# Conditioned attention and a gated low-rank FFN: folding the conditioning weight into the projections and running attention over pairs of batches

## The chip, the cores and the metric

The kernel runs on one core of one Trainium2 chip. The metric is device time in microseconds (us), the median of several runs; less is better. A profile is one execution taken by the hardware profiler. Its engines are PE (TensorE; PEld is its weight load), DVE (VectorE), ACT (ScalarE), POOL (GpSimd) and SP (SyncE, which issues most transfers).

## What is computed

Eight batches of 256 tokens of 1024 features, all in f32. Every batch has its own low-rank adapter (rank 16) of the conditioning layer and its own matrix for the FFN input:

```python
h = x @ W.T + b + (x @ A[i]) @ Bm[i] * 2          # conditioning, i = itok_B_0_23[batch]
q, k, v = h @ w_q, h @ w_k, h @ w_v               # 32 query heads, 8 key heads, head size 32
o = softmax(q @ k.T / sqrt(32)) @ v
x = x + o @ w_o
g = x @ cond2[j].T                                # j = itok_B_3_7[batch]
x = x + top2_gated_low_rank(g)                    # 4 experts of rank 16, router on g
```

The products that matter run on f32 split into two parts, hi and lo (each rounded to the matmul's f32r format), as hi*hi + hi*lo + lo*hi: three products of TensorE for one. ScalarE writes the hi part by a copy, VectorE the lo part by a subtraction. P = 128 partitions, KT = 8 tiles of 128 features, G = 8 groups of 4 query heads that share a key head.

## The kernel before

It has three stages, each with an instruction stream for every engine; an engine goes through its stream in order and waits at semaphores.

**tokens_stage** computes h for pairs of batches, 512 tokens at a time: `products` (L259) multiplies 8 x 8 weight tiles with x, three times, 192 products of 512 columns per pair. `psU` (L281) is the adapter's first factor, `low_rank` (L265) its second. ScalarE adds the bias while it copies h out (L212), SP stores it to h_scratch in DRAM. The q, k and v weights are split meanwhile.

**attend_stage** goes over batches b and, in each, over the 8 groups g: step n = 8b + g. `project` (L646, L643 for v) multiplies h of one batch (256 columns) with a weight block of 128 columns ("unit": q0 to q7, k0, k1, v0, v1) in 24 products, through two PSUM banks. In step n TensorE issues: the first half of q unit g, scores 0 and 1 of step n-1, the second half, scores 2 and 3 of n-1, then transposed scores and outputs of earlier steps and the turn (a small transposition of the row maxima). k0 stands at the head of step 0, v0 and v1 at the end of step 2, k1 at the end of step 3. The stages of a step are:

- `scores` (L661): q times k, by rows of queries, only for the row maxima; VectorE's `maxima` (L578) reduces them. The two banks make score tile i wait for the maximum of tile i-2.
- the negated maxima are turned (L694), copied (L525) and laid by SP (L445) into rows 96 and 97 of q_stack, so that `scores_t` (L673), two steps later, yields transposed scores less the maximum, which ScalarE exponentiates (`exp`, L508).
- `outputs` (L687): probabilities times v, and times ones for the denominators; `copy_o` (L595) copies both to SBUF; SP stores them to o_scratch and den_scratch.
- q is held as a stack of 32 rows each: hi (`copy_q`, L500, ScalarE), lo (L568, VectorE) and hi again (L572, VectorE); k likewise (L480, L550, L486). h of the next batch is loaded and split (L411, L418) in the steps of this one.

**finish_stage** goes over batches. Denominators are loaded together, inverted (L987), stored, and loaded again per batch, broadcast, as o_scale (L832); `scale_o` (L977) multiplies o with them, `scale_hi` and `scale_lo` split it. `w_o_tile` (L1124) is the output projection, `cond_row` (L1139) multiplies router and expert matrices into cond2, the rest (psX, psY) is the gated FFN. The W_o weights are split in the last steps of attention (`ahead_scalar`, `ahead_vector`, steps s = 4 to 7 of the last batch), through a ring of three buffers that VectorE frees.

Of the kernel before, what the change touches and what calls it, by code (L numbers as in the profile page):

```python
# [7 lines left out]
P = 128  # L29
# [8 lines left out]
E = 4  # L38
# [14 lines left out]
RING = 3  # L53
W_TILES = KT
QKV_TILES = NQKV // P
WO_TILES = KT


def f(ap):

    return ap.bitcast(F32)


class Weights:


    def __init__(self, nc, sb, sem):
        self.nc = nc
        self.raw = sb("weight_raw", [P, RING, D])
        self.landed = [sem(f"weight_landed{i}") for i in range(RING)]  # L70
        self.hi_done = sem("weight_hi_done")
        self.lo_done = sem("weight_lo_done")

    def load(self, eng, n, src):
        if n >= RING:
            eng.wait_ge(self.lo_done, n - RING + 1)
        dst = self.raw[:, n % RING]
        if len(src.shape) == 3:
            dst = dst.rearrange("p (k c) -> p k c", c=src.shape[2])
        eng.dma_start(dst, src).then_inc(self.landed[n % RING], 16)  # L80

    def split_hi(self, act, n, hi):
        act.wait_ge(self.landed[n % RING], 16 * (n // RING + 1))
        self.nc.scalar.activation(hi, self.raw[:, n % RING], ACT.Copy).then_inc(self.hi_done, 1)

    def split_lo(self, dve, n, hi, lo):
        dve.wait_ge(self.hi_done, n + 1)
        dve.tensor_tensor(lo, self.raw[:, n % RING], f(hi), ALU.subtract).then_inc(self.lo_done, 1)  # L88
# [6 lines left out]
def tokens_stage(nc, sem, weights, wq, ahead, load_qkv, xT, idx, WT, bias, lora_A, lora_B, hT):  # L95

    SLOTS = 4
    BANK = [0, 1, 2, 3, 4, 5, 6, 3]
    AB_DMAS = 8
    st = Stage()  # L100
    with ExitStack() as ctx:
        def sb(name, shape, dt=F32):
            return ctx.enter_context(nc.sbuf_tensor(name, shape, dt))

        sb("qkv_head", [P, 4, 2, D])
        w_hi, w_lo = sb("w_hi", [P, KT, D], F32R), sb("w_lo", [P, KT, D], F32R)
        x_raw = sb("x_raw", [P, KT, T2])
        x_hi, x_lo = sb("x_hi", [P, KT, T2], F32R), sb("x_lo", [P, KT, T2], F32R)
        idx_sb = sb("idx_sb", [1, B], I32)
        bias_sb = sb("bias_sb", [P, KT])  # L110
        a_raw = sb("a_raw", [P, 2, KT, R])
        a_hi, a_lo = sb("a_hi", [P, 2, KT, R], F32R), sb("a_lo", [P, 2, KT, R], F32R)

        b_raw = sb("b_raw", [96, 2, D])
        b_stack = sb("b_stack", [96, 2, D], F32R)
        u_stack = sb("u_stack", [96, 2, T], F32R)
        h_out = sb("h_out", [P, SLOTS, T2])
        psH = ctx.enter_context(nc.psum_tensor("psH", [P, 7, T2], F32))
        psU = ctx.enter_context(nc.psum_tensor("psU", [P, T2], F32))

        idx_landed, bias_landed = sem("idx_landed"), sem("bias_landed")
        x_landed = [sem(f"x_landed{k}") for k in range(KT)]
        ab_landed = sem("ab_landed")
        zeroed = sem("zeroed")
        x_hi_done, x_lo_done, x_used = sem("x_hi_done"), sem("x_lo_done"), sem("x_used")
        ab_hi_done, ab_lo_done = sem("ab_hi_done"), sem("ab_lo_done")
# [8 lines left out]
    def both(ap):  # L135
        return ap.rearrange("p (b t) -> p b t", b=2)

    def sync(sp):
        def load_x(pair, k):
            sp.dma_start(both(x_raw[:, k]), xT[bass.ds(2 * pair, 2), :, k].rearrange("b p t -> p b t")  # L140
                         ).then_inc(x_landed[k], 16)
# [1187 lines left out]
```

## Time and profile before

| | us |
|---|---|
| median of 3 runs | 1232.97 (1232.5 to 1234.92) |
| the profiled execution | 1233.04 |
| its span | 1231.4 |
| PE busy | 1136.6 (92%) |
| DVE busy | 720.4 (59%) |
| ACT busy | 475.1 (39%) |
| 16 DMA engines | 120.26 MB, 98 GB/s on average |

The span runs from the first to the last instruction; 1.6 us lie around it. The token stage takes the first 228 us, attention goes to 889, the finish to the end. Busy PE is not PE at its peak, since products are pipelined and overlap in the records: the pace of a row of products is better read from the distance of their starts.

### The profile page before, as it was taken

To read this page: it belongs to the slowest core of one execution; us is meant where nothing else is said; L and a number is where in the kernel's file an instruction comes from. 1 tells how busy PE (TensorE), PEld (TensorE's weight loads), DVE (VectorE), ACT (ScalarE), POOL (GpSimd) and SP (SyncE) were. 2 spreads that over 40 slices of the span, in tenths; PEclk is the share of its full clock that TensorE was granted. 3 is DMA by queue.
4 is the path that set the end of the run, shared out by engine and by line. 5 is a ranking of instruction groups with operands and counts; after the bars stand their busy time and mean duration, and the time that the engine had idled before them with its cause. 6 is when DMAs were issued, how large, how long until landed. Compare 5 with 4: busy or idle time off the path is not lost.

```text
span 1231.4 us, 23057 instructions
## 1 busy us (share of the span) xinstructions
PE 1136.6 (92%) x8592; PEld 911.4 (74%) x8592; DVE 720.4 (59%) x1434; ACT 475.1 (39%) x911; POOL 55.4 (5%) x99
## 2 busy tenths in 40 slices
PE   6999999788998999989989899897689999999996
PEld 5788888676776766767667677674379898988895
DVE  5212122467767677676776767767546666566663
ACT  4223123445445454453454544544322322232320
POOL 2000001100000000000000000001011111111100
PEclk9999999899999999999999999998799999999998
DMA  9341423410100101001010010003486866677530
GB/s 298 96 120 56 133 70 102 137 57 33 54 11 15 52 14 48 14 14 48 18 48 14 14 48 19 23 14 125 145 270 172 240 205 208 177 244 224 190 103 35
DMA packets 60418, 120.26 MB, mean 98 GB/s; under 512 B 8660, under 2 KB 43860, under 8 KB 56276
## 3 DMA queue, kind: packets, MB, share of 16 engines
q1 hardware_dynamic: 47124, 71.41, 19.0%
q0 software_dynamic: 13248, 48.24, 12.4%
q8 instruction: 29, 0.48, 0.2%
q14 instruction: 17, 0.14, 0.0%
HBM read 93.41 MB, written 25.69 MB: 97 GB/s over the span
## 4 chain that ended last, share of the span: by engine, by line
PE 62%; ACT 13%; DVE 11%; issue 7%; DMA 5%; SPq 1%; ACTq 0%; DVEq 0%; POOL 0%; POOLq 0%
PE psW L1124 13%; PE psH L259 13%; PE psP L646 9%; PE psG L1139 7%; ACT q_stack L500 5%; ACT probs L508 5%; PE psP L643 4%; PE psS L661 4%; DVE nmax L578 4%; PE psO L687 4%; PE psT L673 3%; DMA o_scale<-rden_scratch 3%; PE psX L1161 2%; DVE o_sb L595 2%; PE psU L281 2%
## 5 line engine op out<-in xcount | busy, mean ns | idle before, releaser
L646 PE MATMUL psP<-h_hi,wq 128*128 128x256 f32 x1280 | 259.8, 289 | 22.5 <-DVE h_lo L418 16.3
L646 PEld LDWEIGHTS psP<-h_hi,wq 128*128 128x128 f32 x1280 | 210.1, 193 | 46.4 <-issue 25.4
L508 ACT ACTIVATE probs<-psT 128x512 f32<-128x512 f32 x256 | 138.9, 594 | 248.4 <-PE psT L673 247.0
L1124 PE MATMUL psW<-wq 128*128 128x256 f32 x1536 | 197.6, 284 | 0.0
L1124 PEld LDWEIGHTS psW<-wq 128*128 128x128 f32 x1536 | 191.6, 191 | 5.3 <-issue 0.6
L578 DVE TENSOR_REDUCE nmax<-psS 128x2 f32<-128x512 f32 x256 | 164.4, 684 | 41.7 <-PE psS L661 40.9
L646 PE MATMUL psP<-h_lo,wq 128*128 128x256 f32 x640 | 181.8, 284 | 0.0
L568 DVE TENSOR_TENSOR q_stack<-psP,q_stack 32x256 fp32r<-32x256 f32 x256 | 107.4, 419 | 102.3 <-ACT q_stack L500 100.5
L932 ACT ACTIVATE cond_hi<-cond_raw 128x1024 fp32r<-128x1024 f32 x64 | 66.8, 1056 | 165.3 <-PE psG L1139 165.3
L661 PE MATMUL psS<-k_stack,q_stack 96*128 96x256 f32 x512 | 98.7, 303 | 29.6 <-DVE nmax L578 25.2
L646 PEld LDWEIGHTS psP<-h_lo,wq 128*128 128x128 f32 x640 | 123.4, 193 | 0.0
L1004 DVE TENSOR_TENSOR cond_lo<-cond_raw,cond_hi 128x1024 fp32r<-128x1024 f32 x64 | 77.6, 1223 | 71.2 <-ACT cond_hi L932 71.2
L259 PE MATMUL psH<-x_hi,w_hi 128*128 128x512 f32 x256 | 101.9, 398 | 9.6 <-DVE w_lo L88 9.3
L661 PEld LDWEIGHTS psS<-k_stack,q_stack 96*128 96x128 f32 x512 | 73.7, 194 | 46.5 <-DVE nmax L578 35.9
L259 PE MATMUL psH<-x_lo,w_hi 128*128 128x512 f32 x256 | 100.8, 394 | 0.0
L259 PE MATMUL psH<-x_hi,w_lo 128*128 128x512 f32 x256 | 100.7, 394 | 0.0
L500 ACT ACTIVATE q_stack<-psP 32x256 fp32r<-32x256 f32 x256 | 95.7, 374 | 6.7 <-PE psP L646 3.3
L673 PE MATMUL psT<-q_stack,k_stack 98*128 98x512 f32 x256 | 90.6, 435 | 4.6 <-ACT probs L508 2.8
L687 PE MATMUL psO<-probs,v_sb 128*32 128x256 f32 x1024 | 73.3, 406 | 0.9 <-DVE o_sb L595 0.9
L687 PE MATMUL psO<-probs,ones 128*32 128x256 f32 x1024 | 70.5, 394 | 0.0
L673 PEld LDWEIGHTS psT<-q_stack,k_stack 98*128 98x128 f32 x256 | 40.5, 196 | 34.1 <-ACT probs L508 28.5
L259 PEld LDWEIGHTS psH<-x_hi,w_hi 128*128 128x128 f32 x256 | 48.7, 190 | 22.3 <-issue 10.7
(101 smaller groups left out, 1360.8 us busy)
## 6 DMA issues: line engine op xcount, KB each, us to landing
cond_raw<-in_cond POOLq DMA_DIRECT2D x64, 512.0 KB, 4.6
x_raw<-in_xT SPq DMA_DIRECT2D x32, 256.0 KB, 5.2
h_scratch<-h_out SPq DMA_DIRECT2D x32, 256.0 KB, 2.5
act_raw<-h_scratch SPq DMA_DIRECT2D x8, 1024.0 KB, 4.9
o_scratch<-o_sb SPq DMA_DIRECT2D x64, 128.0 KB
act_raw<-o_scratch SPq DMA_DIRECT2D x8, 1024.0 KB, 6.5
o_scale<-rden_scratch SPq DMA_DIRECT2D x32, 256.0 KB, 9.4
x_sb<-in_xT SPq DMA_DIRECT2D x8, 1024.0 KB, 6.9
```

The lines of the kernel that those rows point to most:

```text
L259: mm = pe.matmul(psH[:, BANK[m]], w[:, k, cols], x[:, k], start=(first and i == 0), stop=False)
L500: ins = nc.scalar.activation(q_stack[0:32, g % 4, h], psP[32 * h:32 * h + 32, bank, 0:T], ACT.Copy)
L508: nc.scalar.activation(probs[:, g % 2, i % 2, (i // 2) * 512:(i // 2 + 1) * 512], psT[:, i % 2], ACT.Exp, scale=ATT_SCALE).then_inc(exp_do ...
L568: ins = dve.tensor_tensor(q_stack[32:64, g % 4, h], psP[32 * h:32 * h + 32, bank, 0:T], f(q_stack[0:32, g % 4, h]), ALU.subtract)
L578: dve.tensor_reduce(nmax[:, g % 2, 2 * hp:2 * hp + 2, qt], psS[:, i % 2].rearrange("p (h k) -> p h k", h=2), AX.X, ALU.max, negate=True).t ...
L646: mm = pe.matmul(out, wq[:, u, w, k * P:(k + 1) * P], h[:, k], start=first, stop=end)
L661: mm = pe.matmul(psS[:, i % 2, j * T:(j + 1) * T], q_stack[0:96, g % 4, 2 * hp + j, qt * P:(qt + 1) * P], k_stack[0:96, g], start=True, st ...
L673: pe.matmul(psT[:, kt], k_stack[0:98, g, kt * P:(kt + 1) * P], q_stack[0:98, g % 4, 2 * hp:2 * hp + 2].rearrange("p h t -> p (h t)"), star ...
L687: mm = pe.matmul(psO[HD * h:HD * h + HD, hp], ones[:] if hp else v_sb[:, kt, g], probs[:, g % 2, kt, h * T:(h + 1) * T], start=(kt == 0), ...
L1004: dve.tensor_tensor(cond_lo[:, k % SPLIT], cond_raw[:, k % RAW], f(cond_hi[:, k % SPLIT]), ALU.subtract).then_inc(cond_lo_done, 1)
L1124: mm = pe.matmul(out, wq[:, k, w, m * P:(m + 1) * P], o_part(c, o)[:, k], start=(k == 0 and i == 0), stop=(k == KT - 1 and i == 2))
L1139: mm = pe.matmul(psG[0:EC, half], a[:, k], w[:, k % SPLIT, half * 512:(half + 1) * 512], start=(k == 0 and i == 0), stop=(k == KT - 1 and ...
```

## The change

The conditioning is linear, so it is folded into the projection weights. `fold_stage` replaces tokens_stage: it computes W' = W.T times the joined q, k and v weights (1024 x 1536) in three chunks of 512 columns, writes it split into `wq`, and multiplies the second factors of all 8 adapters (8 x 16 = 128 rows) and the bias with the same weights. These small results go through DRAM (b_scratch, bb_scratch).

`attend_stage` now takes x of a pair of batches (512 columns), loaded and split once, and projects it with W'. Each unit ends with one more product, the low-rank part and the bias (`b_stack` times `u_stack`); `project_u` computes u, x times the adapters' first factors. There are 4 pairs of 16 steps; step n handles group g = (n mod 16) // 2 of batch c = n mod 2. `WORK` lists the projection pieces of each step: the first list stands at the head of the step, the second before scores 2 and 3; "a" and "b" are halves of a unit, "+" means the next pair. A unit is finished once its last piece is. Scores of step n, transposed scores of n-1 and outputs of n-2 are in the same step. The third part of the q and k stacks is filled by a transfer (`double`) and no longer by an engine. `normalise` inverts the denominators and multiplies on VectorE each step, so that den_scratch, rden_scratch and o_scale go. The finish is otherwise as it was, unrolled; W_o is loaded whole in the last steps, and split in steps N-2 to N+1, two tiles a step.

The core of the diff (units' copies of u and v, placement in memory, semaphores and removed functions are left out):

```diff
+            load_q(0, k)
+            sp.dma_start(w_raw[:, k], W[k * P:(k + 1) * P]).then_inc(w_landed[k], 16)
+            if k == 0:
+                sp.dma_start(idx_sb[:], idx).then_inc(idx_landed, 16)
+                sp.dma_start(idx2_sb[:], idx2).then_inc(idx_landed, 16)
...
+        for j in range(CHUNKS):
+            if j + 1 < CHUNKS:
+                sp.wait_ge(acc_done, 2 * KT * (j + 1))
+                for k in range(KT):
+                    sp.wait_ge(b_used, KT * j + k + 1)
+                    load_q(j + 1, k)
...
+            if j + 1 < CHUNKS:
+                for k in range(KT):
+                    split_q(j + 1, k)
+            else:
+                ahead(act, True)
+            act.wait_ge(b_used, KT * (j + 1))
+            if j:
+                act.wait_ge(bp_stored, 32 * j)
...
+    def tensor(pe):
+        for j in range(CHUNKS):
+            for k in range(KT):
+                if j == 0:
+                    pe.wait_ge(w_lo_done, k + 1)
+                pe.wait_ge(q_lo_done, KT * j + k + 1)
+                for m in range(KT):
+                    if j and k == 0:
+                        if m < 6:
+                            pe.wait_ge(tile_lo, KT * (j - 1) + m + 3)
+                        elif m == 6:
+                            pe.wait_ge(bp_done, j)
+                        else:
+                            pe.wait_ge(brow_done, j)
+                    for i, (w, q) in enumerate(((w_hi, q_hi), (w_hi, q_lo), (w_lo, q_hi))):
+                        mm = pe.matmul(psF[:, bank(j, m)], w[:, k, m * P:(m + 1) * P], q[:, k],
+                                       start=(k == 0 and i == 0), stop=(k == KT - 1 and i == 2))
+                    if k == KT - 1:
+                        mm.then_inc(tile_done, 1)
+                if j == CHUNKS - 1 and k < KT - 1:
+                    mm.then_inc(w_used, 1)
+            if j == 0:
+                pe.wait_ge(bt_lo_done, 1)
+            pe.wait_ge(tile_lo, KT * j + 1)
+            for k in range(KT):
+                for i, (b, q) in enumerate(((bt_hi, q_hi), (bt_hi, q_lo), (bt_lo, q_hi))):
+                    mm = pe.matmul(psF[:, bank(j, 0)], b[:, k].rearrange("p b r -> p (b r)"), q[:, k],
+                                   start=(k == 0 and i == 0), stop=(k == KT - 1 and i == 2))
+                mm.then_inc(b_used, 1)
+            if j == 0:
+                pe.wait_ge(ones_set, 1)
+            pe.wait_ge(tile_lo, KT * j + 2)
+            pe.wait_ge(acc_done, 2 * KT * (j + 1))
+            pe.matmul(psF[0:2, bank(j, 1)], ones[:, 0:2], acc[:], start=True, stop=True).then_inc(bias_done, 1)
+    st.sync, st.gpsimd, st.scalar, st.vector, st.tensor = sync, gpsimd, scalar, vector, tensor
...
+WORK = [
+    (["v0"], ["v1"]),
+    (["q1"], []),
+    (["v2"], ["v3"]),
+    (["q2"], []),
+    (["q3a"], []),
+    (["q3b"], ["k1a"]),
+    (["k1b"], ["q4a"]),
+    (["q4b"], []),
+    (["q5a"], []),
+    (["q5b"], []),
+    (["q6a"], []),
+    (["q6b"], []),
+    (["q7a"], []),
+    (["q7b"], ["+u"]),
+    (["+k0"], ["+q0a"]),
+    (["+q0b"], []),
+]
...
+        def double(p, u):
+            j = int(u[1:] or 0)
+            if u[0] in "qk":
+                sp.wait_ge(proj_act, unit(p, u) + 1)
+            if u[0] == "q":
+                sp.dma_start(f(q_stack[64:96, j % 2]), f(q_stack[0:32, j % 2])).then_inc(q_dup[j % 2], 16)
+            elif u[0] == "k":
+                sp.dma_start(f(k_stack[32:64, :, 4 * j:4 * j + 4]),
+                             f(k_stack[0:32, :, 4 * j:4 * j + 4])).then_inc(k_dup[j], 16)
...
+        def copy_heads(p, u, to):
+            act.wait_ge(proj_done, unit(p, u) + 1)
+            for h in range(HG):
+                ins = nc.scalar.activation(to(h), both(psP[32 * h:32 * h + 32, bank(p, u)]), ACT.Copy)
+                if h == 1:
+                    ins.then_inc(half_hi, 1)
+            ins.then_inc(proj_act, 1)
...
+        def lows(p, u, to, hi):
+            for h in range(HG):
+                if h == 0:
+                    dve.wait_ge(half_hi, 10 * p + [v for v in SEQ if v[0] in "qk"].index(u) + 1)
+                if h == 2:
+                    dve.wait_ge(proj_act, unit(p, u) + 1)
+                ins = dve.tensor_tensor(to(h), both(psP[32 * h:32 * h + 32, bank(p, u)]), f(hi(h)), ALU.subtract)
+            ins.then_inc(proj_dve, 1)
...
+        def normalise(n):
+            dve.wait_ge(pv_done, n + 1)
+            dve.reciprocal(rden[:], psO[:, 1]).then_inc(rden_done, 1)
+            if n >= 2:
+                dve.wait_ge(o_stored[n % 2], 16 * (n // 2))
+            dve.wait_ge(rden_done, n + 1)
+            dve.tensor_tensor(o_sb[:, n % 2], psO[:, 0], rden[:], ALU.mult).then_inc(o_copied, 1)
...
+        def step(n):
+            p, s = n // STEPS, n % STEPS
+            for part in range(2):
+                for unit_ in finished(n, part):
+                    evacuate(*unit_)
+                if part == 0 and s == 13 and p + 1 < PAIRS:
+                    for k in range(4, KT):
+                        split_x_lo(dve, p + 1, k)
+                if n < N:
+                    maxima(n, 2 * part)
+                    maxima(n, 2 * part + 1)
+            if n < N:
+                split_maxima(n)
+            if n >= 2:
+                normalise(n - 2)
+            if n < N and p + 1 < PAIRS:
+                if s == 8:
+                    split_a_lo(dve, p + 1)
...
+        def project(p, u, half):
+            if half in (None, 0):
+                free(p, u)
+            i = BLOCKS.index(u)
+            out = psP[:, bank(p, u)]
+            for k in range(KT) if half is None else range(4 * half, 4 * half + 4):
+                for n_, (w, part) in enumerate(((0, 0), (0, 1), (1, 0))):
+                    mm = pe.matmul(out, wq[:, i, w, k * P:(k + 1) * P], x[:, k, part],
+                                   start=(k == 0 and n_ == 0), stop=False)
+                if u == "q7":
+                    mm.then_inc(x_used, 1)
+            if half in (None, 1):
+                if u == "k0":
+                    low_rank_ready(p)
+                pe.matmul(out, b_stack[:, i * P:(i + 1) * P], u_stack[:], start=False, stop=True).then_inc(proj_done, 1)
...
+        def step(n):
+            run_work(n, 0)
+            for part in range(2):
+                if part:
+                    run_work(n, 1)
+                if n < N:
+                    scores(n, 2 * part)
+                    scores(n, 2 * part + 1)
+                if 1 <= n <= N:
+                    scores_t(n - 1, 2 * part)
+                    scores_t(n - 1, 2 * part + 1)
+            if n >= 2:
+                outputs(n - 2)
+            if n < N:
+                turn(n)
...
+    def ahead_sync(sp, n):
+        if n == N - 3:
+            sp.wait_ge(before.proj_done, PAIRS * NS)
+            for k in range(KT):
+                sp.dma_start(wo_raw[:, k, 1], Wo[k * P:(k + 1) * P]).then_inc(wo_landed[k], 16)
             sp.dma_start(ra_raw[:], RA).then_inc(const_landed, 16)
```

## Rows read from the trace of the kernel before

**Rows 1.** Windows: length, busy us (count) of PE, PEld, DVE, ACT, POOL; clock, DMA, GB/s

```profile
308.20:776.70 468.50, 437.53 (x3888) 329.58 (x3888) 330.20 (x709) 225.01 (x528) 0.00 (x0) 1.00 0.08 28
...
889.20:1231.40 342.20, 327.11 (x2384) 291.67 (x2384) 203.29 (x414) 92.50 (x97) 31.86 (x60) 0.98 0.62 187
```

**Rows 2.** Chain of waits, whole kernel: start us, us, what

```profile
97.04 21.90 PE psH L259 x96
...
234.64 2.90 PE psP L646 x12
...
508.26 1.44 PE psP L646 x12
...
620.55 3.13 PE psP L646 x24
...
698.63 3.14 PE psP L646 x24
```

**Rows 3.** Timeline of one steady attention step: start us, us, engine, line, operation

```profile
399.87 1.10 PE L661 MATMUL psS<-k_stack,q_stack 96*128 96x256 f32 x4 [0.56 <-DVE nmax L578]
...
400.81 0.63 PE L673 MATMUL psT<-q_stack,k_stack 98*128 98x512 f32 x2
...
401.32 1.08 ACT L508 ACTIVATE probs<-psT 128x512 f32<-128x512 f32 x2 [4.17 <-PE psT L673]
...
401.37 1.07 PE L687 MATMUL psO<-probs,v_sb 128*32 128x256 f32 x16
...
402.94 0.27 PE L694 MATMUL psM<-id_sb,nmax_parts 128*16 128x128 f32 x1
```

**Rows 4.** Timeline of TensorE at the start of the kernel

```profile
9.11 0.77 PE L259 MATMUL psH<-x_hi,w_hi 128*128 128x512 f32 x1 [9.11 <-DVE w_lo L88]
```

**Rows 5.** DMA issues of the whole kernel: transfer, queue, count, size, median us to landing

```profile
h_scratch<-h_out SPq DMA_DIRECT2D x32, 256.0 KB, 2.5
...
o_scale<-rden_scratch SPq DMA_DIRECT2D x32, 256.0 KB, 9.4
```

**Rows 6.** Instructions by line and shape: busy us, mean ns | idle before, releaser

```profile
L568 DVE TENSOR_TENSOR q_stack<-psP,q_stack 32x256 fp32r<-32x256 f32 x256 | 107.4, 419 | 102.3 <-ACT q_stack L500 100.5
...
L500 ACT ACTIVATE q_stack<-psP 32x256 fp32r<-32x256 f32 x256 | 95.7, 374 | 6.7 <-PE psP L646 3.3
...
L228 DVE TENSOR_TENSOR x_lo<-x_raw,x_hi 128x512 fp32r<-128x512 f32 x32 | 22.1, 691 | 60.4 <-ACT x_hi L188 60.4
...
L197 ACT ACTIVATE u_stack<-psU 16x512 fp32r<-16x512 f32 x8 | 4.7, 588 | 72.6 <-PE psU L281 72.5
...
L987 DVE RECIPROCAL den_sb<-den_sb 128x448 f32<-128x448 f32 x1 | 2.9, 2943 | 0.0
...
L236 DVE SCALAR_TENSOR_TENSOR u_stack<-psU,u_stack 16x512 fp32r<-16x512 f32 x4 | 2.7, 682 | 66.4 <-ACT u_stack L197 66.4
...
L987 DVE RECIPROCAL den_sb<-den_sb 128x64 f32<-128x64 f32 x1 | 0.6, 552 | 0.2 <-DMA den_sb<-den_scratch 0.2
```

**Rows 7.** Chain of waits, from the last attention output into the finish

```profile
895.85 22.99 DMA o_scale<-rden_scratch
...
922.67 2.74 PE psG L1139 x6
```

**Rows 8.** Windows of time around three waits of TensorE, columns as in the first group

```profile
32.30:34.80 2.50, 0.08 (x2) 0.07 (x2) 2.30 (x2) 0.00 (x0) 0.00 (x0) 1.00 0.99 303
35.30:38.60 3.30, 3.30 (x18) 2.24 (x17) 0.00 (x0) 0.00 (x0) 0.00 (x0) 0.51 0.31 87
829.90:832.60 2.70, 0.00 (x0) 0.00 (x0) 2.70 (x4) 0.00 (x0) 0.88 (x2) 1.00 0.33 92
834.50:837.70 3.20, 3.20 (x27) 1.29 (x23) 1.56 (x5) 2.08 (x6) 0.00 (x0) 0.54 0.41 146
856.20:858.50 2.30, 0.16 (x2) 0.11 (x1) 2.30 (x4) 0.00 (x0) 0.68 (x2) 1.00 0.59 153
858.50:862.90 4.40, 4.20 (x42) 2.00 (x42) 3.31 (x8) 3.08 (x8) 1.97 (x4) 1.00 0.93 293
```

More of the change, by code:

```diff
@@ L51, with columns @@
 AX = mybir.AxisListType
[L53 to L56, printed above, removed]
+BLOCKS = ["k0", "q0", "q1", "q2", "v0", "v1", "q3", "k1", "q4", "q5", "q6", "q7"]
+NB = len(BLOCKS)
+CHUNKS = 3
+CB = NB // CHUNKS
+def columns(block):
+    kind, j = block[0], int(block[1])
+    return {"q": 0, "k": D, "v": D + NKV}[kind] + j * P
 def f(ap):
     return ap.bitcast(F32)
[L64 to L88, printed above, removed]
@@ new lines, in ahead_sync, with ahead_scalar, ahead_vector @@
+    def ahead_sync(sp):
+        sp.wait_ge(before.w_used, 2)
+        for k in range(KT):
+            if k >= 4:
+                sp.wait_ge(x_lo_done, k - 3)
+            load_x(sp, 0, k)
+    def ahead_scalar(act, last):
+        for k in [KT - 1] if last else range(KT - 1):
+            split_x_hi(act, 0, k)
+        if not last:
+            split_a_hi(act, 0)
+    def ahead_vector(dve, last):
+        for k in [KT - 1] if last else range(KT - 1):
+            split_x_lo(dve, 0, k)
+        if not last:
+            split_a_lo(dve, 0)
@@ L877, in sync, with store @@
+        def store(n):
+            sp.wait_ge(y_added, YT * (n + 1))
+            sp.dma_start(outT[n], x_sb[:, n % 2]).then_inc(stored, 16)
+        sp.wait_ge(before.pv_done, N)
+        sp.wait_ge(before.o_copied, N)
+        load_x(sp, 0)
+        load_x(sp, 1)
         for half in range(2):
             sp.dma_start(fb_raw[ER * half:ER * (half + 1)], ffn_B).then_inc(fb_landed, 16)
-        run(batch)(sp)
-        store(B - 1, 1, YT * B)
+        for s in before.o_stored:
+            sp.wait_ge(s, 16 * N // 2)
@@ L901, in gpsimd @@
-        pool.wait_ge(const_landed, 32)
-        slot = pool.value_load(idx_sb[0:1, 0:1], min_val=0, max_val=7)
-        pool.wait_ge(before.proj_done, before.units)
-        for k in range(RAW):
-            row(0, slot, k)
-        run(batch)(pool)
-    def scale_hi(act, n, c):
-        act.wait_ge(o_scaled, n + 1)
-        if not (isinstance(n, int) and n < 2):
-            act.wait_ge(wo_done, KT * (n - 1))
-        nc.scalar.activation(o_part(c, 0), o_raw[:].rearrange("p (k t) -> p k t", t=T),
-                             ACT.Copy).then_inc(o_hi_done, 1)
@@ L963, in batch @@
             nc.scalar.activation(g_sb[:], psG[0:EC].rearrange("p a b -> p (a b)"), ACT.Copy).then_inc(g_copied, 1)
-            if not is_last(n):
-                cond_row(n, 8)
-                cond_row(n, 9)
-        act.wait_ge(const_landed, 32)
-        act.wait_ge(before.pv_done, 2 * before.steps)
-        run(batch)(act)
+            if n + 1 < B:
+                cond_row(KT * (n + 1))
+                cond_row(KT * (n + 1) + 1)
+        act.wait_ge(const_landed, 16)
+        act.wait_ge(before.pv_done, N)
@@ L1101, in batch @@
                                       ALU.subtract).then_inc(fb_lo_done, 1)
-            if not is_last(n):
-                cond_row(n, 8)
-                cond_row(n, 9)
-        run(batch)(dve)
+            if n + 1 < B:
+                cond_row(KT * (n + 1))
+                cond_row(KT * (n + 1) + 1)
+        for n in range(B):
+            batch(n)
         gates(B)
```

1441 lines of the change are left out of this document (660 added, 781 removed).

## The prediction

> **What bounds the kernel now.** I read the stages first [rows 1]. TensorE is busy 438 of 468 us in six batches of attention and 327 of 342 in the finish, VectorE 330 and 203: TensorE bounds both, in attention with least to spare for what waits on VectorE. Next the chain of waits [rows 2], for prices. 96 products of 512 columns take 21.90 us, 0.228 each; 12 of 256 columns take 1.44 us, 0.120 each. The first q0 work of two neighbouring batches starts 78.1 us apart: a step is 9.8 us. Products of attention per batch: 12 units x 24 x 0.120 = 34.6. What else a step holds is in one steady step [rows 3]: scores 8 x 0.12 = 0.96, transposed scores 0.56 twice, outputs 1.0 twice, the turn 0.20, together some 4.1 (with the 0.96 at pace), so 8 steps hold 67 us and 11 us per batch are waits. The step also shows why it works as it does: each q unit comes in two halves, with scores between, so that VectorE has projection work of TensorE beside it.
>
> **The fold.** Removed: 4 x 192 products of 512 columns, the low-rank parts, the store and reload of h. Added: 3 chunks of 192 products, 24 for the low-rank matrix and one for the bias. The first product needs 256 + 512 KB as now, so it starts at 9.1 [rows 4]; as now, the first 13 products run at half the pace, 13 x 0.2 = 2.6 more. Products: 3 x 192 x 0.228 = 131.3, and 3 x 24 x 0.228 = 16.4. The bias product is plain f32; no row has one alone, I take 1.0 (0.23 at least). The reload of the weight chunk waits for the low-rank products, which release it piece by piece: 0.7 for the first, landing 2.5 [rows 5], two splits of at most 0.69 [rows 6], together 4.6 against 5.8 of products still ahead, so it is hidden; what is late is the eighth piece and behind it, on ScalarE and VectorE, the copies of the low-rank and bias rows, which the seventh and eighth product groups wait for: 0.5 each time, up to 4 if loads land in 5. Sum 9.1 + 2.6 + 131.3 + 16.4 + 3.0 + 1.0 = 163.4. Then u (32 x 0.12 = 3.8), k0 and q0 (25 x 0.228 = 5.7 each) and 0.4 for the b_scratch round trip, beside which u and k0 lie: attention's first step starts at 179, with k0 and q0 behind it; now k0 of batch 0 starts at 234.6 [rows 2]. Gain at least 56 us.
>
> **Projection.** A pair needs u 3.8, ten units of 5.7 and four v units of 3.0: 72.8 us, against 2 x 34.6 = 69.1. Wide products gain 240 x 0.012 = 2.9; u and the low-rank products take 6.7. With 16 x 4.07 of the rest, TensorE's work per pair is 138, against 156 that two batches take now. So the question is what waits remain.
>
> **One step, walked.** Time 0 is the end of the turn of the step before. The reciprocal now runs on VectorE each step: between 0.552 us (64 elements) and 2.943 (448) the slope is 6.2 ns, so 256 give 1.75 [rows 6]; with a product of 0.42 (the price of a 256-element row, L568) normalise ends at 2.2. Its cover is the projection at the head; in a step without one it counts. The trace has no 32x512 evacuation: on ScalarE 0.374 (32x256) and 0.588 (16x512) bound it, on VectorE 0.419 and 0.691 (128x512); the 16x512 rows from PSUM, 0.588 and 0.682, are nearest [rows 6] and I take them. From the end of a product to a reader 0.25 (401.32 against 400.81 + 0.23) [rows 3].
> Half a unit, nothing finished (steps 4, 8, 10, 12): projection to 2.7, two scores to 3.2, two transposed scores to 3.8. VectorE takes maxima of 0.64 from 3.2: 3.8, 4.5. The third score waits for the first maximum, the fourth for the second: 4.8; transposed scores 5.4, outputs 7.4, turn 7.6. Length 7.6.
> A finished unit, nothing after it (7, 9, 11, 15): projection to 3.0, scores 3.4, transposed scores 4.0. ScalarE copies heads 3.2 to 5.6. VectorE starts at 4.4, when two heads are copied, and needs 4 x 0.69: 7.2. Behind these, in its queue, are the maxima: 7.85, 8.5. The third score, and behind it all that TensorE has, waits for 7.9: TensorE is idle 3.9 us. Then 8.8, 9.4, outputs 11.4, turn 11.6. Length 11.6. Now this evacuation lies beside the second half of the projection; after, no projection stands between scores 1 and 2.
> Steps 1 and 3 carry a whole unit: 11.6 + 2.7 = 14.3, with the same 3.9 idle. Steps 0 and 2 (v in both parts, no VectorE evacuation): 10.3. Steps 5 and 6 have 2.7 of projection in the gap, so a unit's evacuation still ends last: 11.6. Step 13: VectorE has four x splits left from step 12 (to 5.0), then q7 (7.8), then four more (10.6); u waits for the last, 12.9; u's own five copies alternate between the two engines and end 15.8; maxima 17.1, turn 17.8. Step 14: k0's last product waits for b_stack, loaded only after o of step 11 is stored, 7.2; its evacuation 11.7; length 16.1. Step 1 also waits 0.9 for v0, which ScalarE copies late.
> Sum of a pair: 4 x 7.6 + 4 x 11.6 + 2 x 14.3 + 2 x 10.3 + 2 x 11.6 + 17.8 + 16.1 + 0.9 = 184, against 156. Each of these waits is small; together they are 46 us of 184.
>
> **The total.** Three pairs from 179: less 0.5 for the opening (no outputs in its first steps) 729.6. The last pair has no next one to prepare: steps 0 to 12 take 184 - 17.8 - 16.1 - 11.6 = 138, step 13 11.6, step 14 7.3, step 15 9.1 (two W_o splits, 2.4, uncovered): 896. Drain: outputs, two normalises, four more W_o splits and the first o split on VectorE, 19: 915. Now the finish starts at 889.2 and takes 342.2 [rows 1], of which some 3.5 are a wait behind o_scale (a transfer of 23 us, the next product at 922.7) [rows 7] that goes, with the store, reload and inversion of the denominators: 339. Sum 1254, and 1.6 around the span (1233.04 against 1231.4; the median is 1232.97, so no correction): 1255, with the clock up throughout.
>
> **The clock.** After TensorE had waited 2.5 us (32.3 to 34.8) the granted clock was 0.51 for 3.3 us; after 2.7 us (829.9 to 832.6) it was 0.54 for 3.2; after a wait of 2.3 us it stayed at 1.00 [rows 8]. These are the levels 1.2 and 2.4 GHz. In six batches of steady attention it is 1.00 [rows 1]. After the change there is one of 3.9 us or more in steps 1, 3, 7, 9, 11, 13 and 15, 27 in all. Behind each come outputs, turn and the next projection, which TensorE alone sets: 3.3 us at half speed cost at most 1.65; I take 1.5, some of it lying in the small waits. 27 x 1.5 = 40. Forecast 1255 + 40 = 1295.
> The Trainium skill speaks against this change at this place: "TensorE: Matmul & The Clock Gate", section "HAM oscillation — how this bites in real kernels", says that a wait that recurs between bursts of products makes the clock fall anew each time, so that the warm-up is paid per burst. By that rule the sum is the 1295 above, without it 1255; the trace of before agrees in the two falls shown, and has no recurring one.
>
> **Rivals.** *The clock stays up*: 1255. For it: the falls of before lie in stages with other gaps nearby, and one wait of 2.3 us passed. Against: both of 2.5 and more fell. 0.17.
> *Evacuation priced by instruction, not by element*: if 32x512 copies cost near 0.40, as 32x256 do, and one follows the other closely, a unit ends 1.5 us earlier, the wait is 2.4 us, and the clock mostly stays up. Nine such steps per pair: 184 - 13.5 = 170, total 1255 - 54 = 1201: faster. It decides once the waits of a pair fall by 5.5 us with the clock up. Against it: the 16x512 rows. 0.12.
> *The copy of the low half comes late*: the 96 rows of q are completed by a 256 KB transfer of 32 partitions on SP's queue. It has 8.7 us from the copy to the first score. 256 KB landed in 2.5 us (h_scratch) and, into 32 partitions, in 9.4 (o_scale) [rows 5]; at 9.4 plus issue each of ten units a pair waits 1.3: +50, 1345. 0.10.
> *The fold brings less than it says*: its reloads land late and the clock falls at each chunk: +15, 1310. 0.06.
>
> **How the numbers follow.** Forecast 1295, 0.55 (1275 to 1320). Range 1240 to 1345: it takes in the clock-up case and most of the late copy. A measurement of this kernel tells 0.2% from no change. Faster 0.13, same 0.03, slower 0.84.
>
> **What would show it.** Right: first score product near 180; a pair near 190 to 195 us; in steps 7, 9, 11 TensorE idle for almost 4 us before the third score, released by VectorE's maxima; granted clock near 0.5 after it; the finish 339 long, no o_scale. Wrong: VectorE's 32x512 subtraction at 0.45, a clock of 1.00 throughout attention, a wait of the first score for a transfer, or a pair under 178.

## The result

The changed kernel takes 1326.36 us, median of 4 runs (1319.03 to 1332.95), against 1232.74 (1231.78 to 1234.92) for the kernel before on the same chip: ratio 1.0755, interval 1.0697 to 1.0814, so 7.6% slower. The forecast was 1295, with a range of 1240 to 1345: the sign and the range hold, and the forecast is 31 us too low. The time lies above the 1275 to 1320 us to which the forecast gave 0.55. Beside the experiments below, the kernel before took 1232.3 to 1234.0 us, so that their times can be laid beside each other.

The head of the page of the changed kernel; each digit of the rows below it is a fortieth of the span, in tenths. PEclk is the clock that TensorE was granted: full is 2.4 GHz, and half of it, 1.2 GHz, is the other level:

```profile
span 1324.7 us, 18170 instructions
...
PE 1136.6 (86%) x7446; PEld 868.5 (66%) x7446; DVE 743.7 (56%) x1245; ACT 427.3 (32%) x718; POOL 47.8 (4%) x88
...
PE   7999987978787978788978787978569999999996
...
PEclk9999988989888999888988888898779999999997
```

TensorE is busy for 1136.6 us, to the tenth what it was before, and the span is 93 us longer. That the two sums are equal is chance. The change did save work (7446 products for 8592, the wide ones dearer), but a part of the busy time is now products at half the clock: experiment 3 below runs the same products, waits less, and is busy for 58 us less.

```profile
PE 1078.3 (92%) x7446; PEld 842.1 (72%) x7446; DVE 740.0 (63%) x1245; ACT 421.0 (36%) x718; POOL 48.0 (4%) x88
```

The stages of the changed kernel, as windows (length; busy us and count of PE, PEld, DVE, ACT, POOL; granted clock; DMA), to be laid beside [rows 1]: the fold with the first u, k0 and q0, the four pairs, the finish.

```profile
7.50:179.40 171.90, 169.24 (x738) 136.72 (x739) 89.42 (x125) 48.46 (x77) 10.90 (x15) 1.00 0.25 83
179.40:379.80 200.40, 159.48 (x1035) 113.06 (x1035) 112.16 (x179) 70.61 (x136) 1.07 (x2) 0.86 0.15 38
379.80:577.10 197.30, 161.02 (x1105) 110.61 (x1104) 115.94 (x181) 70.70 (x137) 1.07 (x2) 0.90 0.15 40
577.10:779.00 201.90, 165.66 (x1105) 113.97 (x1104) 115.72 (x181) 70.69 (x137) 0.00 (x0) 0.86 0.14 38
779.00:984.65 205.65, 153.76 (x1088) 101.21 (x1088) 121.24 (x176) 73.48 (x133) 2.12 (x4) 0.86 0.21 65
984.65:1324.70 340.05, 327.42 (x2384) 292.96 (x2384) 187.34 (x405) 89.80 (x94) 31.68 (x60) 0.97 0.48 163
```

The fold did its part: k0 of the first pair starts at 167.99 and not at 234.6 [rows 2], 67 us earlier. Attention lost more than that. A pair takes about 200 us where two batches took 156, and in it TensorE is busy for only 154 to 166 us, at a clock of 0.86 to 0.90 where [rows 1] has 1.00. The finish is what it was (340 for 342).

One step of the kind "a unit finished, nothing after it", step 13 of the last pair (where no next pair is prepared), from the timeline (start us, us, engine, line, operation, idle before and releaser):

```profile
926.30 3.01 PE L694 MATMUL psP<-x_hl,wq 128*128 128x512 f32 x12
...
929.38 0.64 PE L735 MATMUL psS<-k_stack,q_stack 96*128 96x256 f32 x4
929.64 2.40 ACT L506 ACTIVATE q_stack<-psP 32x512 fp32r<-32x512 f32 x4 [2.79 <-PE psP L701]
...
930.86 2.78 DVE L585 TENSOR_TENSOR q_stack<-psP,q_stack 32x512 fp32r<-32x512 f32 x4 [2.17 <-ACT q_stack L506]
...
933.67 2.61 DVE L604 TENSOR_REDUCE nmax<-psS 128x2 f32<-128x512 f32 x4
...
934.42 1.13 PE L735 MATMUL psS<-k_stack,q_stack 96*128 96x256 f32 x4 [3.93 <-DVE nmax L604]
...
936.33 1.94 PE L760 MATMUL psO<-probs,v_sb 128*32 128x256 f32 x16
```

The two scores are in PSUM by 930.0. VectorE is free then, but the next thing in its queue is the evacuation of the projection unit, which needs two copies of ScalarE first: it starts at 930.86 and ends at 933.64, and only then does the maximum start for which TensorE has waited 3.93 us. The 16 output products then take 1.94 us instead of 1.07: the clock has fallen. Over the kernel the waits of TensorE, and of its weight loads, for a maximum are (us in total, times, longest):

```profile
PEld psS L735 <- DVE nmax L604: 138.2, 85, 4.6
...
PE psS L735 <- DVE nmax L604: 105.3, 33, 4.2
```

### The profile page after: what moved, and what is told of

Read it like the earlier page. It is cut to its first block, busy times and chain, and to the rows that moved or that the text cites. A ratio compares the mean times of both kernels' runs of the same rounds, so it can differ in the third digit from the quotient of the medians.

```text
span 1324.7 us, 18170 instructions
## 1 busy us (share of the span) xinstructions
PE 1136.6 (86%) x7446; PEld 868.5 (66%) x7446; DVE 743.7 (56%) x1245; ACT 427.3 (32%) x718; POOL 47.8 (4%) x88
## 3 DMA queue, kind: packets, MB, share of 16 engines
q1 hardware_dynamic: 33424, 72.52, 17.2%
## 4 chain that ended last, share of the span: by engine, by line
PE 75%; DVE 15%; DMA 4%; ACT 3%; issue 2%; SPq 1%; ACTq 0%; DVEq 0%
PE psW L1093 14%; PE psP L694 13%; PE psO L760 12%; PE psF L238 10%; PE psG L1108 7%; DVE q_stack L585 6%; DVE nmax L604 5%; PE psS L735 4%; PE psP L709 3%; PE psT L746 3%; PE psX L1129 2%; ACT q_stack L506 2%; PE psY L1148 1%; DMA x_raw<-in_xT 1%; PE psF L249 1%
## 5 line engine op out<-in xcount | busy, mean ns | idle before, releaser
L694 PE MATMUL psP<-x_hl,wq 128*128 128x512 f32 x960 | 241.1, 403 | 2.5 <-ACT v_sb L527 2.5
L694 PEld LDWEIGHTS psP<-x_hl,wq 128*128 128x128 f32 x960 | 181.3, 194 | 39.8 <-ACT v_sb L527 3.2
L617 DVE RECIPROCAL rden<-psO 128x256 f32<-128x256 f32 x64 | 112.5, 1757 | 125.1 <-PE psO L760 125.1
L585 DVE TENSOR_TENSOR q_stack<-psP,q_stack 32x512 fp32r<-32x512 f32 x128 | 87.8, 686 | 93.6 <-ACT q_stack L506 92.2
L506 ACT ACTIVATE q_stack<-psP 32x512 fp32r<-32x512 f32 x128 | 75.4, 589 | 109.0 <-PE psP L701 107.4
L238 PE MATMUL psF<-q_hi,w_hi 128*128 128x512 f32 x192 | 76.5, 399 | 10.2 <-DVE w_lo L198 7.5
L238 PE MATMUL psF<-q_lo,w_hi 128*128 128x512 f32 x192 | 76.0, 396 | 0.0
L238 PE MATMUL psF<-q_hi,w_lo 128*128 128x512 f32 x192 | 75.7, 394 | 0.0
L760 PEld LDWEIGHTS psO<-probs,v_sb 128*32 128x32 f32 x1024 | 31.8, 130 | 51.9 <-issue 45.6
L760 PEld LDWEIGHTS psO<-probs,ones 128*32 128x32 f32 x1024 | 40.7, 138 | 37.9 <-issue 25.6
```

Of the source, the lines that this page charges most:

```text
L238: mm = pe.matmul(psF[:, bank(j, m)], w[:, k, m * P:(m + 1) * P], q[:, k], start=(k == 0 and i == 0), stop=(k == KT - 1 and i == 2))
L506: ins = nc.scalar.activation(to(h), both(psP[32 * h:32 * h + 32, bank(p, u)]), ACT.Copy)
L585: ins = dve.tensor_tensor(to(h), both(psP[32 * h:32 * h + 32, bank(p, u)]), f(hi(h)), ALU.subtract)
L617: dve.reciprocal(rden[:], psO[:, 1]).then_inc(rden_done, 1)
L694: mm = pe.matmul(out, wq[:, i, w, k * P:(k + 1) * P], x[:, k, part], start=(k == 0 and n_ == 0), stop=False)
L760: mm = pe.matmul(psO[HD * h:HD * h + HD, half], ones[:] if half else v_sb[:, c, kt, g], probs[:, n % 2, kt, h * T:(h + 1) * T], start=(kt ...
```

## The experiments

Step lengths below run from one turn (product of L766) to the next. In the second pair of the changed kernel the steps 0 to 15 take 9.9, 17.2, 9.9, 16.6, 7.6, 13.0, 11.6, 13.1, 7.4, 13.1, 7.4, 13.1, 7.4, 19.7, 16.3 and 13.9 us: 197.

**1. Is it the place of the evacuation in VectorE's queue?** The theory: the maxima stand behind it, and that is the 3.9 us. The rival: VectorE has too much to do, 28 us of reciprocal per pair among it, and moving work within its queue can't help.

```diff
             for part in range(2):
+                if n < N and part == 0:
+                    maxima(n, 0)
+                    maxima(n, 1)
                 for unit_ in finished(n, part):
                     evacuate(*unit_)
                 ...
-                if n < N:
-                    maxima(n, 2 * part)
-                    maxima(n, 2 * part + 1)
+                if n < N and part == 1:
+                    maxima(n, 2)
+                    maxima(n, 3)
```

> Only VectorE's order changes: in each step the maxima of scores 0 and 1 come before the low-half subtractions of a finished unit, those of scores 2 and 3 after them. Theory (the evacuation at the head of VectorE's step holds up the third score): the wait of TensorE before the third score goes; a step that finishes a unit waits only at its turn, 9.7 us instead of 13.1; the clock stays up in all steps but 13; a pair takes some 169 us and the whole 1221. Rival 1 (VectorE's load as a whole is the bound, with its reciprocals): nothing moves, 1326. Rival 2 (the clock is the cause, not the order): the same idle time appears elsewhere and the clock falls as often, above 1290.

Measured 1223.58 us (1219.47 to 1225.93), ratio to the kernel before 0.9922 (0.9896 to 0.9948). Two calls in another place are worth 103 us, and no engine has less work. The steps 7, 9 and 11 take 10.4, 10.7 and 9.4 for 13.1, the pair 170.5. The place is the cause: both rivals would have left the time above 1290. One part of the expectation missed: the clock did not stay up in all steps but 13. Read in windows of 0.5 us it still falls 19 times from the first step to the finish (39 in the changed kernel).

**2. All of the evacuation behind the maxima and their split.** The edit puts `evacuate` of the first part after `split_maxima`, but for step 13.

> As the run with maxima first, and the subtractions come behind all four maxima and their split (except in step 13). Theory: neither the third score nor the turn waits; a step that finishes a unit takes 7.8, the step after it 8.0 since the reciprocal comes late; a pair 158, the whole some 1180. If only the wait before the third score matters and not the turn: as with maxima first, 1221. Rival (VectorE's load): 1326.

Measured 1220.89 us (1218.21 to 1222.66), ratio 0.9899 (0.9864 to 0.9933): no gain over experiment 1 that the ranges tell apart, 41 us short of what I expected. The timeline of step 9 of the second pair says why:

```profile
444.09 0.64 PE L743 MATMUL psS<-k_stack,q_stack 96*128 96x256 f32 x4
444.35 2.40 ACT L506 ACTIVATE q_stack<-psP 32x512 fp32r<-32x512 f32 x4 [2.36 <-PE psP L709]
...
445.28 1.10 PE L743 MATMUL psS<-k_stack,q_stack 96*128 96x256 f32 x4
...
446.78 2.27 ACT L540 ACTIVATE probs<-psT 128x512 f32<-128x512 f32 x4
...
447.43 0.98 PE L754 MATMUL psT<-q_stack,k_stack 98*128 98x512 f32 x2 [1.05 <-ACT probs L540]
```

The third score now comes after 0.5 us. But ScalarE has the same fault: its four copies stand ahead of the exponentials, the first of which starts at 446.78, though its transposed score was there by 445.2. The wait has moved from VectorE's maxima to ScalarE's exponentials. The step is 9.2 us long, where one with the same products and nothing finished takes 7.4.

**3. ScalarE's order as well.**

```diff
             for part in range(2):
+                first = part == 0 and s != 13 and 1 <= n <= N
+                if first:
+                    exp(n - 1, 0)
+                    exp(n - 1, 1)
                 if not late:
                     for unit_ in finished(n, part):
                         evacuate(*unit_)
                 ...
-                if 1 <= n <= N:
+                if 1 <= n <= N and not first:
```

> The kernel with the evacuation after the maxima on VectorE (1220.9 us), and now on ScalarE too: in every step but 13 the first two exponentials stand ahead of the four copies of the finished projection unit. There a finishing step took 9.2 us against 7.5 for a step of the same products with nothing finished, TensorE's third transposed score waiting 1.05 us for the exponential behind the copies. If the place of the copies is all that is left of the price, the steps 7, 9, 11 and 15 shrink to 7.8 to 8.0 and 1 and 3 to 8.5 to 9: 4 x 1.3 + 2 x 1.5 = 8 us a pair, 32 in all, and fewer clock falls: 1185 to 1190 us. If the load of the engines is what counts (ScalarE's and VectorE's sums are not changed), the copies delay the row copy at the end of the step instead and the time stays at 1218 to 1222.

Measured 1178.89 us (1177.88 to 1180.05), ratio to the kernel before 0.9566 (0.9542 to 0.959): 4.3% faster than the kernel before and 147 us faster than the change as it was made. That is 6 us under the lower end of what I expected. Against the changed kernel, nothing but the order in two queues differs. Step 7 of the second pair, a step of the same kind:

```profile
412.90 0.64 PE L747 MATMUL psS<-k_stack,q_stack 96*128 96x256 f32 x4
...
413.82 1.08 ACT L540 ACTIVATE probs<-psT 128x512 f32<-128x512 f32 x2 [3.42 <-PE psT L758]
...
414.11 2.57 DVE L608 TENSOR_REDUCE nmax<-psS 128x2 f32<-128x512 f32 x4
...
414.79 2.39 ACT L506 ACTIVATE q_stack<-psP 32x512 fp32r<-32x512 f32 x4
414.84 1.10 PE L747 MATMUL psS<-k_stack,q_stack 96*128 96x256 f32 x4 [0.84 <-DVE nmax L608]
...
416.35 1.07 PE L772 MATMUL psO<-probs,v_sb 128*32 128x256 f32 x16
...
417.12 2.79 DVE L589 TENSOR_TENSOR q_stack<-psP,q_stack 32x512 fp32r<-32x512 f32 x4
...
419.93 1.76 DVE L621 RECIPROCAL rden<-psO 128x256 f32<-128x256 f32 x1
```

The copies now run beside the later scores and the first outputs, the subtractions beside the outputs and the next projection. The step is 8.4 us long where it was 13.1 (step 9: 7.6), and the outputs take 1.07, at full clock. The longest wait left here, 0.84, is for the maximum, which starts when the normalisation that stands ahead of it ends.

The number came out 6 us low, but not by the sum that I had made. Steps 1 and 3 end at 11.3 and 10.4 us and not at 8.5 to 9, and steps 4, 8, 10 and 12, which finish nothing, grow from 7.4 to 8.0: the late subtractions push the next reciprocal back (here to 419.93), and the maxima of the next step stand behind it. Against that, the clock falls 10 times from the first step to the finish, for 22 in experiment 2.

**4. ScalarE's order alone.** Is each order a cost of its own, or do they hang together? The edit of experiment 3 on the changed kernel, VectorE as it was.

> The changed kernel (1326.4 us) with ScalarE's order alone: the first two exponentials ahead of the four copies, while on VectorE the four subtractions still stand ahead of the maxima. The two edits together with the maxima first brought 1220.9 to 1178.9, 42 us for ScalarE's part. If the two queues' orders are independent costs, the same 42 come here: 1284. If, as I hold, the subtractions trail the copies (the second copy releases the first of them), they now start 1 to 2 us later and the maxima behind them too: in the five steps of a pair that have only a q unit at their head and in 1 and 3 the step grows by 1 to 2 us, 4 x 7 x 1.5 = 42 us more: 1350 to 1370.

Measured 1401.95 us (1398.94 to 1404.97), ratio 1.1359 (1.1291 to 1.1427). The edit that brings 42 us on top of VectorE's order costs 76 without it. The sign is as I held, the size twice to three times the 24 to 44 us that I expected. Step 11 of the second pair:

```profile
542.58 1.08 ACT L540 ACTIVATE probs<-psT 128x512 f32<-128x512 f32 x2 [3.42 <-PE psT L750]
543.55 2.39 ACT L506 ACTIVATE q_stack<-psP 32x512 fp32r<-32x512 f32 x4
544.76 2.79 DVE L589 TENSOR_TENSOR q_stack<-psP,q_stack 32x512 fp32r<-32x512 f32 x4 [3.75 <-ACT q_stack L506]
...
548.32 1.40 PE L739 MATMUL psS<-k_stack,q_stack 96*128 96x256 f32 x4 [5.55 <-DVE nmax L608]
```

VectorE's subtractions trail ScalarE's copies, so the copies' delay (they start 1.9 us after the first score and not 0.3) goes through the subtractions and the maxima to TensorE: the wait is 5.55 us for 3.93. The mean clock is lower too, 0.886 for 0.912 over the kernel; that part I had left out. So the orders are one chain: copies, subtractions, maxima. Of the two edits VectorE's has to come first.

**5. Is it VectorE's load?** The reciprocal is its largest new piece: 1.76 us, 64 times. Here a plain copy stands for it, so that the output isn't normalised.

```diff
-            dve.reciprocal(rden[:], psO[:, 1]).then_inc(rden_done, 1)
+            dve.tensor_copy(rden[:], psO[:, 1]).then_inc(rden_done, 1)
```

> The reciprocal of the denominators is replaced by a copy of the same 128x256 elements, so the division is left out: 1.76 us become about 0.42 in each of 64 steps on VectorE. Theory (it is covered by the projection at the head of the step, but in steps 13 to 15 of the last pair, step 13 and the drain): 1326 less 3 to 10. Rival (VectorE's load is the bound): 64 x 1.3 less, 1240.

Measured 1318.39 us (1316.57 to 1320.2), ratio 1.069 (1.0644 to 1.0736): 8 us off 1326, where the reciprocals are 112 us of VectorE's time. Two of them stand in the chain of the drain, 1.77 us each, and step 13 of the first three pairs is 0.9 to 1.9 us shorter; the steps 7, 9 and 11 keep their 13.1 to 13.7. The load isn't the bound of the changed kernel; the projection at the head covers the reciprocal, as the forecast had it. (With the orders mended this cover becomes thin, as the 0.84 above shows.)

**6. What do the clock's falls cost?** In the idle time of steps 1, 3, 7, 9, 11 and 15, FILL = 22 extra products of 384 columns, of no use to the result, keep TensorE busy. The waits themselves stay.

```diff
                 if part:
                     run_work(n, 1)
+                    if n < N and finished(n, 0) and not WORK[n % STEPS][1] and n % STEPS != 13:
+                        for _ in range(FILL):
+                            pe.matmul(psM[:, 128:512], x[:, 0, 0, 0:P], x[:, 0, 0, 0:384], start=True, stop=True)
```

> The changed kernel with 22 useless products of 384 columns (3.8 us at full clock) put where TensorE waits before the third score, in steps 1, 3, 7, 9, 11 and 15; the result is not used. Theory: the clock no longer falls there, steps 7, 9 and 11 take 11.6 instead of 13.1, and 23 such steps give 35 us: 1291. Rival (the half clock lies only in time that is waited anyway): the steps stay at 13.1, 1326 or, where the filling ends late, more.

Measured 1271.1 us (1269.83 to 1278.77), ratio 1.0328 (1.0282 to 1.0373): 55 us less with 506 products more. So the falls cost 55 us and not the 35 that I expected (the forecast had 40); and the waits with the clock up cost the rest of the way to 1179, 92 us, as the two kernels have about as many falls left, 11 and 10 from the first step to the finish. The second pair of three kernels, from turn to turn (changed, filled, both orders):

```profile
379.57:576.75 197.18, 160.90 (x1107) 110.49 (x1103) 115.82 (x180) 70.70 (x137) 1.07 (x2) 0.90 0.15 40
```

```profile
362.90:546.27 183.37, 171.27 (x1238) 129.21 (x1234) 115.76 (x180) 70.83 (x137) 1.07 (x2) 0.97 0.16 43
```

```profile
340.90:501.78 160.88, 147.55 (x1106) 105.93 (x1102) 114.75 (x181) 68.97 (x138) 1.07 (x2) 0.97 0.18 49
```

VectorE and ScalarE have the same work in all three (115.8, 115.8 and 114.8; 70.7, 70.8 and 69.0), which leaves order and clock. TensorE's own busy time falls from 160.9 to 147.6 with the same products: 13 us of the 36 by which the pair is shorter are products that run at full clock again.

**7. The late rows of the last pair.** In step 15 of the last pair the transfer of the negated maxima, which usually takes 1.75 us, took 8.57, behind eight 512 KB loads of W_o on the same queue. The chain of waits, changed kernel:

```profile
940.67 1.75 DMA q_stack<-nmax_rows
...
950.21 8.57 DMA q_stack<-nmax_rows
...
984.65 5.45 PE psW L1093 x24
```

The edit sends the loads two a step, over steps 13 to 15 and the first of the drain.

> The changed kernel with one edit on SP's queue: the eight 512 KB loads of W_o, issued all at once ahead of the row transfer of the last pair's step 14, go out two a step over steps 13 to 16 instead. In the changed kernel the row transfer stood 9.14 us behind them (949.5 to 958.8) while 2.5 us is usual, and the last step was 15.1 us where 9 to 10 was forecast. If the queue is the cause, that step loses 5 to 6.5 us, the next loses 1 to 2, and the finish, whose first products want W_o, starts no later: 1318 us, ratio to the changed kernel 0.994. If the rows only fill a time in which TensorE would have waited for something else, 1326. If W_o now comes late for the finish, 1330 or more.

Measured 1323.28 us (1320.74 to 1325.43), ratio 1.0728 (1.07 to 1.0755); by the ranges no difference. The chain of this kernel:

```profile
959.20 1.76 DMA q_stack<-nmax_rows
...
970.79 4.68 DMA wo_raw<-in_Wo
975.50 1.07 ACT wq L917
...
984.20 4.89 PE psW L1095 x24
```

The rows come in time and the last step shrinks from 15.1 to 10.8, but now W_o is waited for, and the finish starts at 984.20 against 984.65. In both orders that were run, what goes last on the queue is waited for, and the finish starts at the same time. That no order would do better is not shown: the last two loads now go out at 970, behind the store of the outputs, and loads ending a step earlier were not tried. Both orders and this edit together:

> Both edits: evacuation behind the maxima on VectorE and behind the first two exponentials on ScalarE, and W_o's loads two a step over steps 13 to 16 of the last pair. If the two are independent, the time is that of the scalar-order kernel less 6 to 9 us: 1178 to 1184. If the engines' load is the bound, 1212 to 1222.

1180.67 us (1179.45 to 1182.44), ratio 0.9583 (0.9558 to 0.9607), the same as without it. The orders' gain stands; nothing is added. The number lies in the 1178 to 1184 expected only because the kernel with both orders was itself faster than expected: the 6 to 9 us that the spread loads were to bring did not come.

**8. The wait for x in step 13.** With both orders mended the longest idle time of TensorE in a pair is the one for the second half of the next pair's x:

```profile
467.20 0.42 PE L687 MATMUL psP<-x_hl,a_stack 128*32 128x256 f32 x1 [4.32 <-DVE x_hl L383]
```

Filled with 26 products of 384 columns ahead of the fifth block of u:

> The scalar-order kernel (1178.9 us) with 26 extra products of 384 columns, of no use to the result, in step 13 of each of the first three pairs, ahead of the fifth column block of the next pair's u, where TensorE idled 4.3 us for x (4.32 behind the split of x) and then ran the rest of u at 1.2 GHz (0.21 us a product of 256 columns for 0.11, from 467 to 472). The wait stays as long. If the lost clock after it is a cost of its own, 24 products lose 0.10 us less each, 2.4 us a pair, and what follows may gain 1 more: 1179 less 7 to 10, 1169 to 1172 us. If the half clock hides behind the x split that follows, or the filling runs past the wait, 1177 to 1181.

Measured 1176.71 us (1171.75 to 1181.56), ratio 0.9539 (0.9485 to 0.9593): not told apart from 1178.9. In the profiled execution u's products run at full clock again, as the windows over them show (clock 0.63 with both orders from 467.2, 1.00 filled from 466.1):

```profile
467.20:474.20 7.00, 7.00 (x42) 5.04 (x46) 2.43 (x4) 2.23 (x5) 0.00 (x0) 0.63 0.01 2
```

```profile
466.10:472.40 6.30, 5.19 (x51) 3.65 (x52) 2.33 (x4) 2.74 (x5) 0.00 (x0) 1.00 0.00 1
```

But step 13 of that pair shrinks only from 19.7 to 18.8: the filled TensorE now waits for the splits of x that follow (0.77 us for the last, at 468.31), which the half clock had hidden. A fall is worth less where something else is due next.

## Why the prediction was right, and where it was short

- *Products and fold.* Forecast 163.4 for the end of the fold, 179 for the first step; measured 163.2 to 164.2 for the bias product and 179.4. Two errors cancel: the first product started at 7.55 and not at 9.1, and the wait behind the reload of the weight chunk, forecast as 0.5 each time, took 1.25 and 1.35 us, at the place that was named (the copy of the low-rank rows; the loads landed in 4.3).
- *The price of an evacuation.* From [rows 6] I took 0.588 and 0.69 for the 32x512 forms that the trace of before did not have. The profile after has them, and they decide between 11.6 and 10 us per step:

```profile
L506 ACT ACTIVATE q_stack<-psP 32x512 fp32r<-32x512 f32 x128 | 75.4, 589 | 109.0 <-PE psP L701 107.4
...
L585 DVE TENSOR_TENSOR q_stack<-psP,q_stack 32x512 fp32r<-32x512 f32 x128 | 87.8, 686 | 93.6 <-ACT q_stack L506 92.2
...
L617 DVE RECIPROCAL rden<-psO 128x256 f32<-128x256 f32 x64 | 112.5, 1757 | 125.1 <-PE psO L760 125.1
```

  The rival by which they cost 0.40 (1201 us) fell with them; the reciprocal, worked out at 1.75 from a slope, is 1.76.
- *The step, walked.* Experiment 6 shows the steps with the clock up (but for step 13, where it still falls): 7.4 where 7.6 was forecast, 11.5 for 11.6, 14.2 and 15.1 for 14.3 and 15.2, 9.95 for 10.3, 19.2 for 17.8, 16.3 for 16.1; the second pair 183.4 for 184. The idle time of 3.93 us was forecast as 3.9. This part, which holds the sign, was right.
- *The late copy* (1345 us): the transfers that complete the stack landed in 2.9 us, and no score but the very first waited for one (2.69 us, before 185.07). It fell.
- *The clock.* Forecast: 27 falls of 3.3 us, 1.5 each, 40 in all. This is the term that was mis-sized, in number and in length. Read in windows of 0.5 us, the granted clock falls below full 37 times in the four pairs, and 28 falls less in experiment 6 are worth 55 us, 2.0 each. What the other 9 cost no run shows by itself. In the second pair the clock is down for 3.5 to 4 us in steps 5, 7, 9 and 11 and for 7 us or more in steps 1, 3, 13 and 15. Against the filled kernel the steps 7, 9 and 11 lose 1.6 each, as forecast; 1, 3 and 15 lose 2.1 to 2.4; and step 5, where I had no fall, 1.5 (it has none in the filled kernel, though its own waits are not filled; the same holds for the fall in the very first step). Of the 37 falls, 16 are of the short kind and 21 of the long. The two falls of before on which I built, 3.3 and 3.2 us long [rows 8], were both of the short kind. One of the long ones, behind 3.3 us without a product:

```profile
271.00:274.30 3.30, 0.00 (x0) 0.00 (x0) 3.08 (x5) 2.38 (x5) 0.00 (x0) 0.83 0.31 67
274.30:281.30 7.00, 6.60 (x43) 3.68 (x44) 3.48 (x7) 1.35 (x3) 0.00 (x0) 0.59 0.04 8
```

  The first three pairs make 16.6 of the missing 31 us (599.6 from the first step to the last pair, 583 forecast), most of it in this way: laid beside the filled kernel, the falls of these pairs cost 46.7 us (44.0 from the first turn on and 2.7 in the first step), where 21 falls of 1.5 are 31.5. The Trainium skill, "TensorE: Matmul & The Clock Gate", section "HAM oscillation — how this bites in real kernels", states of recurring waits for DMA that TensorE starts cold after each. It held here for waits on another engine: the fall came back pair after pair, and filling the waits took 55 us off.
- *The end of attention.* The last pair with its drain took 205.7, where the forecast has 166 + 19 and six falls, 194. The step that failed is "step 15 9.1", measured 15.1: the W_o loads were costed by their splits and not by their transfer. Eight loads of 512 KB and the rows share a queue, and in both orders of experiment 7 the time goes into one of the two waits. Step 14 took 9.5 for 7.3 and the drain 20.7 for 19.
- *The rest.* Finish 340 for 339; what lies around the span 1.7 for 1.6.

So the sum of the errors is 16.6 in three pairs, 11.7 in the last and 2 elsewhere, 30 of the 31 us. The working has three slips of its own, none of which bears on the outcome: three pairs of 184 less 0.5 from 179 end at 730.5 and not 729.6, the steps 0 to 12 of the last pair come to 138.5 and not 138, and the terms named for the rest of a step (0.96, twice 0.56, twice 1.0, 0.20) add up to 4.3 and not 4.1, which makes TensorE's work of a pair 141 and not 138.

The mechanism was right, and experiments 1 and 6 show it. That the time fell inside the range is in part luck: the room above 1320 was made for the late copy, which did not come, and the clock and the last pair filled it.

Why the change is slower, then: the fold brings 67 us to the first k0, and attention with the finish gives back 160. Experiment 3 splits this. Of the 160, 147 are the order of the evacuation in two queues, some 55 of them through the clock, and 13 are left. In the kernel before, the order for the q units was the right one: there `exp` stands ahead of `copy_q` in the scalar step, and `maxima` and `split_maxima` ahead of it in the vector step (lines 520 to 527 and 602 to 610). The change put the projection at the head of the step and its evacuation with it. With the orders mended a pair takes 160.9 us against 156 for two batches: pairs, the single burst and the head position together gain nothing in attention, and the whole 4.3% is the fold's. What holds the pair at 160.9 is, by its waits and apart from the 138 to 141 us of work, the maxima by a little in six steps, the x of step 13, the b_stack of step 14 and the turn of step 13 (second pair, both orders: waited for, us in total, times, longest).

```profile
PE psP L687 <- DVE x_hl L383: 4.3, 1, 4.3
PE psS L747 <- DVE nmax L608: 3.7, 6, 0.8
PE psP L713 <- DMA b_stack<-bb_scratch: 1.8, 1, 1.8
PE psM L778 <- DVE nmax_parts L616: 1.7, 1, 1.7
```

I did not try to start these transfers earlier; x has only one buffer, which q7 reads until step 13.

## What to carry to other kernels

When work is moved in one engine's program, walk what it releases in every other queue: in this kernel a unit's evacuation (2.8 us on VectorE, behind two copies of ScalarE) cost 0.2 to 1.0 us in its step and 0.6 in the next where it stood behind the work that the critical engine waits for, and 3.9 us of waiting plus a clock fall ahead of it. Put the short link of the recurrent chain (maxima, exponentials) first in each queue, and the bulk evacuation behind it; and look at the queues as one chain, since an edit that brings 42 us after the other was made cost 76 us without it. Before moving a transfer out of the way of another, ask whether both fit in the stretch at all.

## What the runs showed of the hardware

- On 32 partitions a copy or subtraction from PSUM costs by its free elements: 0.589 us (ScalarE) and 0.686 us (VectorE) for 512, against 0.374 and 0.419 for 256 [rows 6]. A subtraction of 128x512 takes 0.691 there and one of 16x512 from PSUM 0.682: in these forms the partitions hardly count.
- The granted clock after a wait of 3.3 to 3.9 us stays down for two different lengths in one kernel, near 3.5 to 4 us and near 7, for waits of like length (3.93 us both in step 1 of the second pair, with the long fall, and in step 13 of the last, with the short one). I had expected one length. What decides between them the runs do not show. A wait of 2.69 us, before the very first score, was followed by a fall in the changed kernel and by none in the filled one.
- 506 extra products made a kernel 55 us faster, and once (experiment 8) brought nothing that can be told, where another engine's work was due next.
